# Three rounded blocks of w2 in the expert layer, and low parts loaded only for a new expert: one change to a Perceiver-layer kernel

## Time and profile before

| | |
|---|---|
| median of 3 runs | 1295.25 us (1295.1 to 1296.33) |
| the profiled execution | 1296.94 us, its span 1295.2 us |
| TensorE busy | 1268.2 us, 98% of the span |
| VectorE busy | 749.9 us, 58% |
| ScalarE busy | 358.0 us, 28% |
| DMA | 391.42 MB, mean 302 GB/s |
| stage A | to about 590 us |
| stage B | about 600 to 830 us |
| router, scatter, shared expert | to about 985 us |
| expert stage | about 985 to 1237 us |

### The profile page before, as it was taken

The page is one execution under the profiler, slowest core; times in us unless marked ns, Lnnn a source line. Parts: engine busy times, 40 slices in busy tenths (PEclk is TensorE's granted clock), DMA queues, the critical chain, the costliest instruction groups (busy, mean ns, idle before and its releaser), DMA issues.

```text
span 1295.2 us, 21508 instructions
## 1 busy us (share of the span) xinstructions
PE 1268.2 (98%) x7571; PEld 829.1 (64%) x7572; DVE 749.9 (58%) x1404; ACT 358.0 (28%) x632; POOL 168.6 (13%) x173
## 2 busy tenths in 40 slices
PE   6999999999999999999999999999998999999999
PEld 3444444444444444467888888899986677777743
DVE  4456566554554545468878888666434444444456
ACT  2312212221121211326444444532312323223200
POOL 1000000000000000003100004504324000000054
PEclk9999999999999999999999999999999999999999
DMA  9999999999999999803467752223689898998897
GB/s 358 411 419 416 414 416 418 418 419 419 419 419 412 400 391 394 324 18 149 169 253 272 293 216 78 92 72 123 234 291 305 280 298 293 310 307 289 281 348 250
DMA packets 119699, 391.42 MB, mean 302 GB/s; under 512 B 11744, under 2 KB 34272, under 8 KB 115424
## 3 DMA queue, kind: packets, MB, share of 16 engines
q1 hardware_dynamic: 114528, 374.00, 76.3%
q0 software_dynamic: 5120, 16.78, 3.6%
HBM read 332.54 MB, written 58.20 MB: 302 GB/s over the span
## 4 chain that ended last, share of the span: by engine, by line
PE 92%; DMA 4%; DVE 2%; issue 1%; SPq 1%; ACT 0%; POOL 0%; ACTq 0%; POOLq 0%; DVEq 0%
PE ps L2016 14%; PE ps L1904 13%; PE ps L2088 12%; PE ps L2078 10%; PE ps L2371 5%; PE ps L1979 4%; PE ps L1862 3%; PE ps L2469 2%; PE ps L2461 2%; PE ps L2387 2%; PE ps L2390 2%; PE ps L2393 2%; PE ps L1994 2%; PE ps L2374 2%; DMA arena<-ctx_n 2%; PE ps L2377 1%
## 5 line engine op out<-in xcount | busy, mean ns | idle before, releaser
L2016 PE MATMUL ps<-arena 128*64 128x512 f32 (+1 forms) x832 | 192.3, 594 | 0.0
L1904 PE MATMUL ps<-arena 128*64 128x512 f32 (+1 forms) x1024 | 178.3, 504 | 1.8 <-DVE arena L1172 1.1
L2088 PE MATMUL ps<-split 128*128 128x256 f32 x1344 | 170.7, 285 | 1.2 <-DVE split L1371 1.2
L2088 PEld LDWEIGHTS ps<-split 128*128 128x128 f32 x1344 | 163.7, 191 | 5.7 <-issue 3.5
L799 ACT ACTIVATE arena<-ps 128x512 f32<-128x512 f32 (+2 forms) x132 | 67.3, 523 | 337.9 <-PE ps L1979 180.2
L1904 PEld LDWEIGHTS ps<-arena 128*64 128x64 f32 x1024 | 65.4, 137 | 122.2 <-issue 119.7
L2016 PEld LDWEIGHTS ps<-arena 128*64 128x64 f32 (+1 forms) x832 | 58.3, 137 | 112.4 <-issue 111.7
L1268 DVE SCALAR_TENSOR_TENSOR arena<-arena,hbar 128x512 f32<-128x512 f32 x128 | 90.5, 749 | 67.9 <-PE ps L1979 66.3
L2078 PE MATMUL ps<-split 128*128 128x512 f32 x384 | 96.7, 400 | 1.1 <-DVE arena L1439 1.1
L1242 DVE TENSOR_TENSOR F<-arena,ps 128x512 f32<-128x512 f32 x16 | 11.0, 688 | 135.9 <-ACT split L844 135.9
L702 POOL TENSOR_TENSOR arena<-arena,row_b 128x512 f32 (+1 forms) x16 | 20.2, 1268 | 474.0 <-DVE arena L1142 446.4
(11 more groups left out here) (245 smaller groups left out, 1995.9 us busy)
## 6 DMA issues: line engine op xcount, KB each, us to landing
arena<-ctx_t SPq DMA_DIRECT2D x122, 800.5 KB, 17.6
arena<-ctx_n SPq DMA_DIRECT2D x96, 768.0 KB, 14.1
arena<-ctx_n SPq DMA_DIRECT2D x32, 1024.0 KB, 15.5
split<-parts_low SPq DMA_DIRECT2D x26, 768.0 KB, 7.1
high<-parts_low SPq DMA_DIRECT2D x39, 512.0 KB, 4.9
moe_in<-zero SPq DMA_DIRECT2D x3, 3328.0 KB, 13.5
low_late<-parts_low SPq DMA_DIRECT2D x13, 768.0 KB, 7.0
moe_out<-arena SPq DMA_DIRECT2D x39, 256.0 KB, 4.5
```

Of the source, the lines that this page charges most:

```text
L1904: last = mm(bank(n)[S * h:S * (h + 1), 0:w], qT[:, k, S * h:S * (h + 1)], ctxT[h][:, k, at_j:at_j + w], start=(k == 0), stop=(k == KD - 1))
L2016: last = mm(bank(7)[S * h:S * (h + 1), :], ET[0:w, c, S * h:S * (h + 1)], ctxN[h][0:w, c, :], start=(c == 0), stop=(c == JC - 1))
L2088: last = mm(dst[:, 2 * P * m:2 * P * (m + 1)], w[a][:, k, c], tokens[b][:, k, :], start=(k + i == 0), stop=(k == KD - 1 and i == 2))
```

## The change: what it does

`KB` becomes 3, so each group's product with w2 has one raw block and nine rounded passes in place of two and six. What ScalarE and VectorE copy and subtract for the parts of the inner result follows `KB`, and a w2 low part is 768 KB. The third place of `low_w2` moves to a free stretch of SBUF. The sets of stage B are formed anew: 48 blocks in 12 sets of four, each set in two pieces (two loads, two stores of the high and two of the low parts).

The low parts of both layers are loaded by a conditional DMA from g = 3 on: the transfer is made only if the expert of group g is another than that of group g-3, whose low part lies in the same place. The condition is worked out on SyncE from two further `value_load`s.

```diff
-KA, KB = 3, 2
-NS = E + E // 2
+KA, KB = 3, 3
+BLOCKS = [(0, e, k) for e in range(E) for k in range(KA)] + [(1, e, k) for e in range(E) for k in range(KB)]
+NS = len(BLOCKS) // KD
...
-        for _ in range(3):
+        for _ in range(2):
             low_w2.append(as_split(carve(KB, D), all_high))
         yg = [carve(D) for _ in range(2)]
         assert used[0] == WS + KD * FS + KF * D
+        at(WS + 2 * KF * D + D)
+        low_w2.append(as_split(carve(KB, D), all_high))
...
             def store_part(n, parts, stage):
-                w, e, k = set_of(n)
-                sp.dma_start(parts[w].rearrange("(e p) f -> p e f", p=P)[:, e, :],
-                             of_set(n, stage[n % 2]).bitcast(F32).rearrange("p (e k) n -> p e (k n)", k=k)
-                             ).then_inc(parts_out, 16)
+                for w, e, lo, hi, place in pieces(n):
+                    sp.dma_start(parts[w][P * e:P * (e + 1), D * lo:D * hi],
+                                 stage[n % 2][:, place:place + hi - lo, :].bitcast(F32).rearrange("p k n -> p (k n)")
+                                 ).then_inc(parts_out, 16)
...
-            def load_low(e, i):
+            def other_expert(g):
+                return expert_of(g) != expert_of(g - 3) if g >= 3 else None
+
+            def load_low(g):
+
+                i = g % 3
+                if g >= 3:
+                    sp.wait_ge(low_back[i], 16 * (g // 3))
                 sp.dma_start(low_w[i].bitcast(F32).rearrange("p k n -> p (k n)"),
-                             parts_low[0][bass.ds(e * P, P), :]).then_inc(low_back[i], 16)
-
-            def load_low2(g, e):
+                             parts_low[0][bass.ds(expert_of(g) * P, P), :], cond=other_expert(g)
+                             ).then_inc(low_back[i], 16)
+
+            def load_low2(g):
                 if g > 0:
                     sp.wait_ge(low2_back, 16 * g)
                 sp.dma_start(low_w2[g % 3].bitcast(F32).rearrange("p k n -> p (k n)"),
-                             parts_low[1][bass.ds(e * P, P), :]).then_inc(low2_back, 16)
+                             parts_low[1][bass.ds(expert_of(g) * P, P), :], cond=other_expert(g)
+                             ).then_inc(low2_back, 16)
...
             for g in range(GT):
                 if g + 1 < GT:
-                    e = expert_of(g + 1)
                     if g > 1:
                         sp.wait_ge(y_done, g - 1)
-                    load_low2(g + 1, e)
+                    load_low2(g + 1)
                 if g + 3 < GT:
-                    e = expert_of(g + 3)
                     sp.wait_ge(in_done, g + 1)
-                    load_low(e, g % 3)
+                    load_low(g + 3)
```

More of the change, by code:

```diff
@@ L284, in perceiver_layer @@
         assert used[0] == WS + KD * FS + KF * D
+        at(WS + 2 * KF * D + D)
+        low_w2.append(as_split(carve(KB, D), all_high))
+        assert used[0] <= ARENA, used[0]
         at(0)
@@ L419, in perceiver_layer, with pieces @@
         mix_ready, out_sem = sem("mix_ready"), sem("out_sem")
-        def of_set(n, stage):
-            return stage[:, 0:(KA if n < E else 2 * KB), :]
+        def pieces(n):
+            found = []
+            for place, (w, e, k) in enumerate(BLOCKS[KD * n:KD * (n + 1)]):
+                if found and found[-1][0:2] == [w, e]:
+                    found[-1][3] = k + 1
+                else:
+                    found.append([w, e, k, k + 1, place])
+            assert len(found) == 2
+            return found
         def xg_of(g):
@@ L496, in _ @@
             w_src = [w.rearrange("e (k p) n -> p e k n", p=P) for w in (w1t, w2t)]
-            def set_of(n):
-                w, e = (0, slice(n, n + 1)) if n < E else (1, slice(2 * (n - E), 2 * (n - E) + 2))
-                return w, e, (KA, KB)[w]
             def load_raw(n):
-                w, e, k = set_of(n)
-                for i in range(e.start, e.stop):
-                    j = (i - e.start) * k
-                    sp.dma_start(stage_raw[n % 2][:, j:j + k, :], w_src[w][:, i, 0:k, :]).then_inc(raw_in[n % 2], 16)
+                for w, e, lo, hi, place in pieces(n):
+                    sp.dma_start(stage_raw[n % 2][:, place:place + hi - lo, :], w_src[w][:, e, lo:hi, :]
+                                 ).then_inc(raw_in[n % 2], 16)
             def store_part(n, parts, stage):
-                w, e, k = set_of(n)
-                sp.dma_start(parts[w].rearrange("(e p) f -> p e f", p=P)[:, e, :],
-                             of_set(n, stage[n % 2]).bitcast(F32).rearrange("p (e k) n -> p e (k n)", k=k)
-                             ).then_inc(parts_out, 16)
+                for w, e, lo, hi, place in pieces(n):
+                    sp.dma_start(parts[w][P * e:P * (e + 1), D * lo:D * hi],
+                                 stage[n % 2][:, place:place + hi - lo, :].bitcast(F32).rearrange("p k n -> p (k n)")
+                                 ).then_inc(parts_out, 16)
             load_raw(0)
@@ L527, in _ @@
                 store_part(n, parts_low, stage_low)
-                sp.wait_ge(parts_out, 32 * (n + 1))
+                sp.wait_ge(parts_out, 64 * (n + 1))
                 if n + 2 < NS:
@@ L597, in load_low2 @@
                 sp.dma_start(low_w2[g % 3].bitcast(F32).rearrange("p k n -> p (k n)"),
-                             parts_low[1][bass.ds(e * P, P), :]).then_inc(low2_back, 16)
-            e = expert_of(0)
+                             parts_low[1][bass.ds(expert_of(g) * P, P), :], cond=other_expert(g)
+                             ).then_inc(low2_back, 16)
             sp.wait_ge(x3_out, 48)
-            load_low(e, 0)
+            load_low(0)
             load_w2(ARENA + KD * D, 7, 8)
@@ L620, in _ @@
             load_w2(2 * KD * D, 2, 3)
-            e = expert_of(1)
             sp.wait_ge(xgT_ready, 1)
@@ L627, in _ @@
             sp.wait_ge(shlo_used, 1)
-            load_low(e, 1)
-            e = expert_of(0)
+            load_low(1)
             sp.wait_ge(shared_done, TA)
-            load_low2(0, e)
-            load_low(expert_of(2), 2)
+            load_low2(0)
+            load_low(2)
             for g in range(GT):
                 if g + 1 < GT:
-                    e = expert_of(g + 1)
                     if g > 1:
                         sp.wait_ge(y_done, g - 1)
-                    load_low2(g + 1, e)
+                    load_low2(g + 1)
                 if g + 3 < GT:
-                    e = expert_of(g + 3)
                     sp.wait_ge(in_done, g + 1)
-                    load_low(e, g % 3)
+                    load_low(g + 3)
                     sp.wait_ge(xgT_ready, g + 2)
@@ L936, in round_set @@
             def round_set(n):
-                act.wait_ge(raw_in[n % 2], 16 * (n // 2 + 1 + max(0, (n - E) // 2 + 1)))
-                nc.scalar.activation(of_set(n, stage_high[n % 2]), of_set(n, stage_raw[n % 2][:, :, :]), ACT.Copy
-                                     ).then_inc(high_done, 1)
+                act.wait_ge(raw_in[n % 2], 32 * (n // 2 + 1))
+                nc.scalar.activation(stage_high[n % 2], stage_raw[n % 2][:, :, :], ACT.Copy).then_inc(high_done, 1)
             def stage_b(n, now, last, first=False, second=False, more=True):
@@ L1478, in low_of_set @@
                 dve.wait_ge(high_done, n + 1)
-                v.tensor_tensor(of_set(n, stage_low[n % 2]), of_set(n, stage_raw[n % 2][:, :, :]),
-                                of_set(n, stage_high[n % 2]).bitcast(F32), ALU.subtract).then_inc(low_done, 1)
+                v.tensor_tensor(stage_low[n % 2], stage_raw[n % 2][:, :, :], stage_high[n % 2].bitcast(F32),
+                                ALU.subtract).then_inc(low_done, 1)
             def start_b():
```

## The result

The changed kernel takes 1340.46 us (median of 4 runs, 1337.63 to 1345.29); the kernel before, 1295.28 us. The ratio is 1.0351, with a 95% interval of 1.032 to 1.0382: slower. The prediction was 1338 us. The profiled execution took 1340.84 us, its span 1338.8 us.

A forecast was written before the change was run, and what follows sets the result against it. TensorE bounds the kernel before, SyncE's instruction stream the changed one. From 995.1, 35 iterations of 7.66 us give 1263.2 and passes ending at 1272.1, 42.8 us later; less 0.4, +42.4 us: 1338 us, range 1310 to 1357.

The forecast's parts named there:

- The bound moves to SyncE: Expert stage: SyncE's own work of 7.66 us an iteration exceeds TensorE's 6.13, so SyncE becomes the bound.
- The size of SyncE's work: SyncE's loop: 4.65 us, plus 2.25 for four reads, 0.70 for conditions, 0.06 for a wait: 7.66 us an iteration.
- The condition and the added wait: SyncE's two conditional loads: 0.35 us each, 0.70 an iteration, plus 0.06 us for the wait on `low_back`.
- The path to the end: Group 38's rows asked for at 1263.2 us, landed at 1267.8, its w1 passes ended at 1272.1.
- The start of the stage: Expert stage: larger `low2(0)`, two more reads and a condition move the request for group 3's rows from 992.8 to 995.1.
- stage B: Eight sets grow to four blocks; counted as nothing because TensorE's work hides it, 4.7 us on VectorE without that cover.
- The third block's gain: TensorE's w2 product: three rounded passes for one raw block save 0.18 us a group, 7.0 us over 39 groups.
- The clock: Rival for the expert stage: TensorE's gaps lower its clock, adding 0.1 to 0.3 us a group: 1345 us; chance 0.08.
- The signs in the profile: 222 SyncE reads, iterations of 7.3 to 8.1 us, transposes mostly waiting for rows, TensorE near 80% busy, lower DMA share.

The follow-up runs named there:

- one read: The changed kernel with each group's expert read once by SyncE and kept for both loads and both comparisons: ratio 0.9945, timed again 0.9951.
- all loads: The changed kernel without `cond=` at both loads, so every low part is transferred, with two register reads an iteration: ratio 1.0083, 1314.41 us.
- the reads alone: The kernel before with four more register reads per iteration of SyncE's loop, their values unused: ratio 1.024, 1334.54 us.
- the condition alone: The kernel before with the conditional loads and their six register reads an iteration, `KB` still 2: ratio 1.0228, 1334.77 us.
- rows-first kernel: The changed kernel with one read a group, own semaphores per w2 low place and rows buffer, rows issued before the w1 low part: 0.994, repeated 0.9914.

## Why the prediction was right

**The bound moves to SyncE.** Right, and shown: four unused reads alone give 1.024, their removal with all else kept gives 0.9945.

**The size of SyncE's work.** 7.66 us forecast, 7.49 measured, by errors that cancel; that the time came out within 3 us is in part luck. (a) The work before was put at 4.65 us and is 4.78, since waits outside the 35 iterations were counted into them. (b) A read was put at 0.56 us from the median; 0.62 to 0.63 is what it costs in the loop. The earlier trace rows shows the reason: a median of 270 but a longest of 1132 ns. The mean over the 78 reads of that trace is 331 ns, 0.06 more than the median, and a stream that only sums pays the mean. Four reads were 2.25 us and are 2.50. (c) The condition and the added wait were put at 0.76 and are 7.49 - 7.28 = 0.21 us net: two short instructions a load (40 and 48 ns with a handover each, 0.17), two of them 0.34, one wait of 0.06, less what wasn't foreseen, that a skipped DMA is issued in 0.09 instead of 0.36 us. 30 of 72 loads are skipped, 0.27 x 30 / 35 = 0.23 us an iteration. The prediction said that a skipped transfer saves none of its issue time; that was wrong. 0.34 + 0.06 - 0.23 is 0.17, near the 0.21. What makes 7.62 of 7.49 are 4.4 us of waits in the 35 iterations, which the sum had at nothing. So 0.17 us too much work an iteration (6.0 us in all) stands against 4.4 us of waits and 2.5 us at the start of the stage that were missing.

**The path to the end.** Rows of group 38 asked for at 1263.2, measured 1264.15; L656's successor at 1273.0 where 1272.1 was forecast. The fixed 8.9 us from request to the end of the passes were right (8.86).

**The start of the stage.** Forecast 995.1 for the rows of group 3, measured 997.62. The rows of group 0 were already asked for 2.3 us later (962.59 against 960.26), and from there to those of group 3 it took 2.5 us longer, where 2.3 was forecast. Of the first 2.3 us, 1.0 comes from stage B, counted at nothing. TensorE's timeline there, before and after (the first and the fourth of the projections with 24 passes):

```profile
595.76 3.10 PE L2088 MATMUL ps<-split 128*128 128x256 f32 x24 [1.19 <-DVE split L1371]
...
607.98 3.11 PE L2088 MATMUL ps<-split 128*128 128x256 f32 x24
```
```profile
597.49 3.11 PE L2095 MATMUL ps<-split 128*128 128x256 f32 x24 [1.13 <-DVE split L1378]
...
605.74 3.13 PE L2095 MATMUL ps<-split 128*128 128x256 f32 x24 [0.31 <-DVE arena L1393]
610.73 3.11 PE L2095 MATMUL ps<-split 128*128 128x256 f32 x24
```

12.22 us became 13.24: the first, larger set costs 1.0 us, since at the head of the loop TensorE waits for VectorE (0.31 us here, and 0.6 at L1869 behind it). All three kernels with larger sets whose timeline was read there (the changed one, one read, all loads) show 13.23 to 13.24, those with small ones (the reads alone, the condition alone) 12.27. The steady step is 31.07 us with either, as forecast from the earlier trace rows; a row of the steady loop says nothing of its first turn. The other 1.7 us stood before stage B began. The kernel with the condition alone, whose stages A and B are those of before, has them too (its first projection at 597.79), so no change of the code can be behind them; I take them as scatter between executions.

**The third block's gain.** 6.13 us a group was forecast. Where nothing else was late, in the rows-first kernel, TensorE's transposes of two groups 27 apart are these:

```profile
1051.45 0.60 PE L1875 MATMUL ps<-ident,row_a 128*128 128x128 f32 x4
...
1217.29 0.60 PE L1875 MATMUL ps<-ident,row_a 128*128 128x128 f32 x4
```

165.84 us are 6.14 each, after 6.31 before: 0.17 us a group where 0.18 was forecast. SyncE's step doesn't measure this pace: the rows of groups 3 and 38 are 214.5 us apart in this kernel, 6.13 an iteration, but 214.4 also in the one with `KB` at 2 and one read, whose TensorE needs 6.31.

**The clock.** The rival put it at some microseconds. The granted clock in the window after is 0.96, and TensorE is busy in 211 of 240 us, 88% instead of the 80% expected. Passes in slow stretches take longer. A window behind a gap of 1.33 us (from 1095.7 to 1097.1):

```profile
1100.00:1102.00 2.00, 2.00 (x6) 1.60 (x5) 0.00 (x0) 0.00 (x0) 0.00 (x0) 0.52 0.35 131
```

0.52 of 2.4 GHz is the lower level, 1.2, in nearly all of it. Six instructions ran in it, where the same two microseconds of the kernel before hold twelve at a clock of 1.00. SyncE waited only 0.2 us for TensorE in the whole stretch (the row of its waits above), so TensorE's slower passes filled gaps and didn't set the pace.

**The signs in the profile.** The transposes wait for rows 25 times in the 240 us from 1010 on, which hold some 32 groups: most, as forecast. The register read of the page (the Trainium skill, "DMA: Bandwidth & Descriptors", "Latency and other measured facts": about 600 ns as a floor) isn't borne out for the instruction itself, which took 260 ns at least and 268 in the median of 222. It is near what a whole read, three instructions with their handovers, costs here; taken so, it would have sized the term better than the median did.

## What to carry to other kernels

An engine that only issues DMAs shows no busy time, and can still be the bound. Take the step from one iteration to the next, subtract its waits (only those that lie inside the steps), and compare with the pace of the busiest engine before adding a register read, a comparison or an issue to its stream; count each from start to start and by the mean. A load spared by a condition is cheap, but read what the condition needs once and keep it. When the stream is near its pace, look for its waits for landings too: they add to its work.

## What the runs showed of the hardware that was not expected

- A register read of one value from SBUF on SyncE costs 0.62 to 0.63 us from start to start in this loop, though the medians of its three instructions add up to 0.44 us; reads of the same place in a row aren't merged (222 in the trace, as many as the code asks for).
- With TensorE at 6.31 us a group, one gap of 1.99 us at the start of the stage cost about as much again (2.06 us) in slower passes behind it.
